# Waiting for the landing of each short run of indirect DMAs on GpSimd

## What is computed

```python
# layer 0: a gated message of each edge, summed by src
z = concat([x[src], x[dst], edge_attr], 1) @ W.T + b          # 106250 x 256
z = (z - mean(z, 0)) * rsqrt(var(z, 0) + eps) * gamma + beta   # over all edges
agg = zeros.at[src].add(sigmoid(z[:, :128]) * softplus(z[:, 128:]))
x1 = layernorm(x + (x + agg))
# layer 1: mean over the neighbours, by dst
local_mean = segment_sum(x1[src], dst) / max(count, 1)
fd = tanh(norm(x1 - local_mean))
h  = x1 + 0.2 * (relu(x1 @ W1 + b1) @ W2 + b2) * fd
out = layernorm(x1 + layernorm(h) * gamma1 + beta1)
```

## Time and profile before

| | |
|---|---|
| median of three runs | 3949.55 us (3946.03 to 3959.84) |
| span of the profiled execution | 5481.6 us, mean granted TensorE clock 0.784 |
| the profiled execution's time outside the span | not shown by the profile |
| busy | TensorE 3436.3 us, VectorE 2979.6, GpSimd 2626.3, ScalarE 2242.8 |
| scatters, line 367 | 830, at 66 to 1711 us |
| first gather, line 1245 | 272, at 3567 to 3951 us |
| second gather, line 1255 | 608, at 4249 to 5388 us |

### The profile page before, as it was taken

How to read it: one execution, slowest core, us unless ns; L and a number is a source line. 1 busy time by engine, 2 the same in 40 slices (tenths; PEclk the granted TensorE clock), 3 DMA queues, 4 the chain that set the end, 5 groups by cost and what they waited for, 6 DMA issues and landing times. The chain is left out here.

```text
span 5481.6 us, 84513 instructions
## 1 busy us (share of the span) xinstructions
PE 3436.3 (63%) x18854; PEld 2395.6 (44%) x18855; DVE 2979.6 (54%) x7781; ACT 2242.8 (41%) x6113; POOL 2626.3 (48%) x2634
## 2 busy tenths in 40 slices
PE   6745666666656888888888885661175555455542
PEld 2312222222223666666666664551165445445542
DVE  7975555555655333333333337971198555455547
ACT  1405555555654444444444448971197000000002
POOL 3775444444553555555555550077600544545542
PEclk8957777778877888888888887885587777777766
DMA  5322222122221666656666575463443221222213
GB/s 166 110 88 67 60 65 63 59 61 65 61 68 56 191 190 186 195 186 188 188 191 188 184 173 222 169 241 114 130 194 87 58 49 47 53 53 53 56 41 39
DMA packets 314711, 638.06 MB, mean 116 GB/s; under 512 B 54382, under 2 KB 188567, under 8 KB 306551
## 3 DMA queue, kind: packets, MB, share of 16 engines
q0 software_dynamic: 99440, 246.85, 16.9%
q1 hardware_dynamic: 172984, 266.76, 15.7%
q10 hardware_dynamic: 42192, 123.38, 6.1%
HBM read 424.53 MB, written 212.24 MB: 116 GB/s over the span
## 5 line engine op out<-in xcount | busy, mean ns | idle before, releaser
L367 POOL DMA_INDIRECT rec_d<-arena x830 | 887.8, 1070 | 815.8 <-issue 520.7
L853 POOL DMA_INDIRECT arena<-b_tab,arena x880 | 839.2, 954 | 730.4 <-DVE arena L874 405.8
L767 PE MATMUL psum<-arena 128*128 128x440 f16 x3360 | 776.5, 390 | 369.5 <-DVE arena L626 140.8
L626 DVE TENSOR_SCALAR arena<-iota_t,arena 128x880 f16<-128x880 f16 x840 | 516.1, 664 | 545.9 <-remote 320.5
L461 ACT ACTIVATE arena<-arena 128x128 f16<-128x128 f16 x1680 | 568.5, 388 | 469.9 <-remote 333.1
L767 PEld LDWEIGHTS psum<-arena 128*128 128x128 f16 x3360 | 344.2, 106 | 803.5 <-DVE arena L626 322.1
L1569 PE MATMUL psum<-arena,x_sb 128*128 128x129 f32 x2304 | 398.3, 347 | 454.2 <-DVE x_sb L1456 320.9
L964 PE MATMUL psum<-weT,arena 128*128 128x256 f32 x1760 | 627.6, 443 | 31.9 <-DVE arena L874 21.9
L1448 DVE TENSOR_TENSOR arena<-psum,arena 128x258 f32 x880 | 375.3, 426 | 476.9 <-remote 282.2
L1569 PEld LDWEIGHTS psum<-arena,x_sb 128*128 128x128 f32 x2304 | 375.7, 257 | 480.4 <-issue 192.3
L1255 POOL DMA_INDIRECT arena<-x_tab,arena x304 | 299.9, 987 | 556.1 <-DMA x_tab<-arena 295.9
(11 more groups left out here) (251 smaller groups left out, 5920.5 us busy)
## 6 DMA issues: line engine op xcount, KB each, us to landing
z_d<-arena ACTq DMA_DIRECT2D x220, 512.0 KB
arena<-z_d SPq DMA_DIRECT2D x44, 2560.0 KB
arena<-rec_d SPq DMA_DIRECT2D x220, 260.0 KB
arena<-in_edge_attr SPq DMA_DIRECT2D x83, 640.0 KB
arena<-early_d SPq DMA_DIRECT2D x34, 516.0 KB
arena<-b_tab,arena POOLq DMA_INDIRECT x880
rec_d<-arena POOLq DMA_INDIRECT x831
early_d<-arena POOLq DMA_DIRECT2D x9, 1032.0 KB
```

Of the source, the lines that this page charges most:

```text
L367: nc.gpsimd.indirect_dma_start(rec_rows, bass.IndirectOffsetOnAxis(e_idx[:, s, k:k + 1], 0), e_buf[:, s, k, :], None).then_inc(s_es[s], 16)
L626: nc.vector.tensor_scalar(hot_tile[:, s, :].rearrange("p (a b) -> p a b", b=TILE_RUN), iota_t[:, :, 0:TILE_RUN], tile_f[:, bass.ds(t, 1)], ...
L767: last = nc.tensor.matmul(bank(4 + 2 * k + h)[:, 0:HALF], hot_lane[:, s, k, :], hot_tile[:, s, h * HALF:(h + 1) * HALF], start=start, stop ...
L853: nc.gpsimd.indirect_dma_start(bg[:, s, k, :], None, b_tab, bass.IndirectOffsetOnAxis(rec[:, s, k, H:H + 1].bitcast(I32), 0)).then_inc(s_b ...
```

## The change

GpSimd gets waits on its own transfers. In part 1 it waits, before the first of a group's ten scatters, until the group before has landed entirely, and before the sixth until the first five have landed. In the first and the second gather it waits in the same way before the first and the fifth of a group's eight rows. Each wait asks for the full count of all DMAs of that semaphore so far, so nothing of GpSimd's is in the air when the next run of five, or of four, begins. The first three groups of scatters are taken out of the loop. Nothing else is changed, and the gather of the z stage isn't.

```diff
--- before.py
+++ after.py
@@ -359,18 +359,27 @@
                 nc.gpsimd.tensor_copy(identb[:], ident[:]).then_inc(s_const, 1)
                 pool.wait_ge(s_const, N_CONST + 2)
 
-                def scatter(it1, s):
+                RUN_IN = 5
+
+                def scatter(it1, s, first=False):
                     pool.wait_ge(s_el[s], it1 * 16)
                     pool.wait_ge(s_er[s], it1 * 3)
+                    if not first:
+                        pool.wait_ge(s_es[(s - 1) % IN_SLOTS], (it1 if s > 0 else it1 - 1) * (16 * G_IN))
                     settle(pool, s_turn)
                     for k in range(G_IN):
+                        if k == RUN_IN:
+                            pool.wait_ge(s_es[s], it1 * (16 * G_IN) - 16 * (G_IN - RUN_IN))
+                            settle(pool, s_turn)
                         nc.gpsimd.indirect_dma_start(rec_rows, bass.IndirectOffsetOnAxis(e_idx[:, s, k:k + 1], 0),
                                                      e_buf[:, s, k, :], None).then_inc(s_es[s], 16)
 
                 pool.wait_ge(s_tail0, 16)
                 pool.wait_ge(s_lz, 16 * len(LAST_BY_SP))
                 pool.wait_ge(s_lza, 16 * len(LAST_BY_ACT))
-                with pool.Fori(0, N_GROUPS_IN // IN_SLOTS) as it:
+                for s in range(IN_SLOTS):
+                    scatter(1, s, first=(s == 0))
+                with pool.Fori(1, N_GROUPS_IN // IN_SLOTS) as it:
                     for s in range(IN_SLOTS):
                         scatter(it + 1, s)
                 for g in range(N_GROUPS_IN // IN_SLOTS * IN_SLOTS, N_GROUPS_IN):
@@ -1131,6 +1140,7 @@
         x1e = flat[:, 0:EARLY_BLOCKS * (H + 1)].rearrange("p (b f) -> p b f", f=H + 1)
         x_ring2 = flat[:, 0:2 * G * (H + 1)].rearrange("p (s k f) -> p s k f", s=2, k=G)
         XS = 4
+        RUN = 4
 
         def ring_slot(s):
 
@@ -1242,6 +1252,9 @@
                     if g >= XS and g % 2 == 0:
                         pool.wait_ge(s_be[g // 2 % 2], g // XS * 16)
                     for k in range(G):
+                        if k % RUN == 0 and g + k > 0:
+                            before = g if k > 0 else g - 1
+                            pool.wait_ge(s_xe[before % XS], (before // XS + 1) * (16 * G) - (16 * (G - k) if k > 0 else 0))
                         nc.gpsimd.indirect_dma_start(ring_slot(g % XS)[:, k, :], None, x1_tab,
                                                      bass.IndirectOffsetOnAxis(l1_idx[:, g * G + k:g * G + k + 1], 0)).then_inc(s_xe[g % XS], 16)
                     if g >= 2 and g % 2 == 0:
@@ -1250,8 +1263,11 @@
                 for i in range(2):
                     pool.wait_ge(s_be[i], len(range(i, EARLY // 2, 2)) * 16)
 
-                def rows(s):
+                def rows(s, use):
                     for k in range(G):
+                        if k == RUN:
+                            pool.wait_ge(s_xe[s], use * (16 * G) + (EARLY_IN[s] - 16 * (G - RUN)))
+                            settle(pool, s_turn)
                         nc.gpsimd.indirect_dma_start(ring_slot(s)[:, k, :], None, x1_tab, bass.IndirectOffsetOnAxis(gi[:, s, k:k + 1], 0)).then_inc(s_xe[s], 16)
 
                 pool.wait_ge(s_xs, 48)
@@ -1263,15 +1279,19 @@
                         wait(pool, s_sg, 24 * (2 * use) + (8 * s - 80))
                     else:
                         wait(pool, s_sg, 24 * (2 * use) + (8 * s - 72))
+                    last = (s - 1) % XS
+                    pool.wait_ge(s_xe[last], (use if s > 0 else use - 1) * (16 * G) + EARLY_IN[last])
                     settle(pool, s_turn)
-                    rows(s)
+                    rows(s, use)
 
                 groups(pool, gather, None, 4 * ROUNDS, XS, head=XS)
                 for n in range(4 * ROUNDS, DIRECT):
                     pool.wait_ge(s_gi, n + 1)
                     before = n - XS
                     pool.wait_ge(s_sg, 8 * (3 * (before // 2) + 2 + before % 2 if before < 4 * ROUNDS else 2 * ROUNDS + before + 1))
-                    rows(n % XS)
+                    last = (n - 1) % XS
+                    pool.wait_ge(s_xe[last], ((n - 1) // XS + 1) * (16 * G) + EARLY_IN[last])
+                    rows(n % XS, n // XS + 1)
 
             @block.scalar
             def _(act):
```

## The result

The changed kernel takes 4752.12 us (median of four runs, 4747.16 to 4757.37) against 3947.79 for the kernel before: ratio 1.2051, 95% interval 1.2028 to 1.2073, slower by 804 us. The forecast was 4380, with a range to 4560; the sign was right and the size was not.

A forecast was written before the change was run, and what follows sets the result against it. The prediction took GpSimd as close to the bound, and as the bound in the average stage. Terms of 35 + 163 + 39 + 275 = 512 us gave 4461; between that and 4260 it forecast 4380 us, range 3850 to 4560.

The forecast's parts named there:

- sum of stages at the undisturbed pace: Whole kernel: busiest engine's time per stage, 3622 us, or 3966 with 10% idle added, 0.4% above the median.
- stalls without the profiler: Sign of a wrong prediction: VectorE's 10.5 us standstills in placement also without profiling; time then falls with the span.
- span between 5100 and 5500: Changed kernel's profiled execution: expected no longer than the 5481.6 us before, while a plain run gets longer.
- price of a wait: Every added wait: 2.09 us idle less the usual 0.30 gap, 1.79 us, from one gather row.
- cover of the scatters: Ranks and placement: ScalarE's 41 us a round and the ranks' pace hide part; 35 + 163 us come out.
- cover of the first gather: First gather: 435 us of messages and normalisation hide most of 474 us; 39 come out, bounds 0 and 72.
- term of + 275: Second gather, average stage: GpSimd is the bound, 76 groups take 1041 us against 766.
- Halving: Whole forecast: 4380 us, between 4461 at the profile's GpSimd pace and 4260 at a pitch nearer 1.10 us.
- All waits bare and dear: Rival, all 384 waits: 1.79 + 0.46 us at each, 864 us, 4810 in all; chance 0.03.
- The waits are covered: Rival, no change: pitch below 1.0 us and cheap landings hide the second gather's waits, 3950 us; chance 0.07.
- Cured stalls: Rival, faster: waits break GpSimd's long rows and cure stalls in the changed stages, 3825 to 3698 us; chance 0.20.

The follow-up runs named there:

- e0_before: The kernel before, unchanged, profiled once more: 3953.54 us, with a profiled span of 3946.0 us.
- e3: The kernel before with only the 152 waits in the second gather, two a group: 4296.97 us against 3956.49.
- e13: The kernel before with only one wait a group (76) in the second gather: 4121.45 us against 3955.73.
- e14: The kernel before with one wait a group in all three places, for the group before the last: 3953.31 us against 3955.73.
- e4: The kernel before with only one wait a group in the second gather, in a batch with stalls: 5253 us against 5471.58.
- e8: One wait a group in the second gather only, run in the other batch with stalls: 5301 us against 5296.41 for the kernel before.
- e9: The kernel before with one wait a group in all three places, for the group before the last, among stalls: 5502 us against 5296.41.
- e2_only_first: The kernel before with only the 67 waits in the first gather: 4120.87 us against 3956.49.

## Why the prediction came out as it did

**What a plain run is: half right.** The sum of stages at the undisturbed pace (3966) matched the median, and e0_before has no stalls anywhere, so the step from 5481.6 to 3950 was sound. That it matched to 0.4% was luck: I had the z stage at 1224 us (1102 over 0.9) where it takes 1121, and the average stage at 687 where it takes 771, and the two nearly cancel. The reading was wrong too: I called the difference the profiler's, and it is the execution's. The forecast named stalls without the profiler as a sign that it is wrong; some executions have them, those of the median don't. With that falls the expectation of a span between 5100 and 5500: it is 4755.6.

**The price of a wait: right for the scatters, too low for the gathers.** 1.79 us came from one row. Measured: 1.85 for the scatters (305 / 165), 2.24 in the second gather (340 / 152). There the landing row gives 2.06 to 2.08 of it and the rest, some 27 us in all, are idle times that I didn't trace one by one.

**The first step that failed: the cover of the scatters.** I gave a round of placement 41 us of ScalarE, against 38.2 of GpSimd, and took 163 + 35 us. In e0_before no scatter but one waits for ScalarE (0.3 us in all), and ScalarE waits for them instead. GpSimd's busy time in the two halves, ranks and placement (length, busy us, clock):

```profile
66.00:367.00 301.00, 243.25 (x186) 0.78 0.36 109
367.00:1210.00 843.00, 646.75 (x644) 0.97 0.35 99
```

With the gap of 0.30 behind each, 186 scatters of 1.31 us fill the first and 644 of 1.00 us the second. Three groups of placement take 39.3 us, and the 41 of ScalarE were 37 of work over an assumed 0.9. There was nothing to hide a wait under, not in the ranks either, where I had charged 35 us of 53. Each wait is bare: 305 us, 107 more than forecast.

**The second: the cover of the first gather.** I let 34 groups at 10.1 us run under 435 us of messages, so that 39 us came out. But beside working engines a gather is not 1.26 us: in e0_before 272 of them take 448 us. They end at 3074 us, while the stores of the last x1 were issued by 3030, and the second gather begins 7 us after their end. In e0_before's view of the line (duration ns min/median/max) the median is that of a quiet stage, and the longest ten times as much:

```profile
L1245 POOL DMA_INDIRECT arena<-x_tab,l_idx x144: 947/954/9813, 2626.4 to 3072.7; - x144
```

What the long ones have in common stands in the trace. When the longest starts, VectorE works on two operands in the chip's memory (line 1484):

```profile
3056.25 6.68 DVE L1484 TENSOR_TENSOR arena<-arena 128x6272 f32<-128x6272 f32 x1
3056.31 9.81 POOL L1245 DMA_INDIRECT arena<-x_tab,l_idx  x1 [0.31 <-issue]
```

All 24 others over 2.5 us lie beside an instruction of line 1380, which has two such operands too, and end 0.81 to 0.84 us after it. There was no cover at all, and beside the loads of z a landing took longer: 164 us, 125 more. The stalled profile hid both, as it had slowed just the engines that disturb a gather (VectorE 129 us busy in 385, against 396 in 448).

**The second gather: right in its mechanism.** GpSimd was the bound, at 771 us against my 766 and then 1120 against 1041; the term of + 275 was 340, by the price.

**Halving: wrong.** I averaged 4461 with a sum for a GpSimd pitch of 1.10 us, to mend 2.4% in my sum of stages. These 2.4% are 95 us, and they were the z stage's, which I had 103 us too long. GpSimd's usual pitch is 1.27 and 1.26 in e0_before as in the profile before, and with the long descriptors its mean is higher, 1.38 for the scatters and 1.65 in the first gather (its 17 stores included). So "0.95 + 0.30 at every one of some 2500 DMAs", with which I argued against the rival of covered waits, was not what the trace had. The halving took off 81 us. With 107, 125 and 65 the four make 378 of the 372 us by which I was low.

**The rivals.** "All waits bare and dear" (4810, to which I gave 0.03) is the one that came about, at 2.09 us a wait instead of 2.25. "The waits are covered" fell: e3 and e13. "Cured stalls" fell for executions without stalls, e14 above all; for those with stalls its mechanism was seen in one stage (e4 and e8), and whether the changed kernel gains there stays open, as it never ran in such a batch. What makes an execution stall stays open too. The runs show only that it lasted for a whole batch, and each batch has one chip.

**The Trainium skill's rule held.** The Trainium skill ("DMA: Bandwidth & Descriptors", "Rules for kernel authors") advises to wait late on a DMA's semaphore. The fixed cost of about 2.0 us that the same page gives for a GpSimd DMA ("Anatomy of one DMA — SWDGE (gpsimd) path") made 768 us for 384 waits, an estimate; 804 were measured. Another page of the Trainium skill, "SBUF — State Buffer" (section "SBUF: two separate sides"), says that a VectorE instruction with two inputs in SBUF, the chip's memory, holds a pair of ports for its whole length against a GpSimd instruction that reads SBUF. The long descriptors beside line 1380 agree with it, 24 of the 25 over 2.5 us in e0_before. The timeline of the changed kernel has them as well; no run here takes VectorE's work away to show it.

```profile
3021.97 2.82 DVE L1400 SCALAR_TENSOR_TENSOR arena<-arena 128x2560 f32<-128x2560 f32 x1 [1.04 <-ACT arena L1323]
...
3022.06 3.56 POOL L1258 DMA_INDIRECT arena<-x_tab,l_idx  x1 [0.30 <-issue]
```

## What to carry to other kernels

When a profile's span is far from the time, profile again before pricing anything: a second profile of the same kernel would have put right three of the four terms. An engine with no idle time but its fixed gaps is the bound. Here every wait on its own transfer then cost the full landing, in proportion to the count, and a wait for the group before the last was free. Whether there are only fixed gaps is read from the mean over a stage, not from a few regular rows: the earlier trace rows had 229 us for 177 descriptors where a row has 0.97 each. Cover is to be read from a trace in which the covering work runs at its real pace, since that work also slows what it covers.

## What the runs showed of the hardware

- A landing waited out by the issuer adds 1.85 us to a scatter into DRAM, 2.2 to a gather into the chip's memory, and up to 6.4 us of idleness was seen beside loads of 2.5 MB; the scatters' writes into DRAM were not the dearer ones.
- A gather's descriptors, 0.95 us else, took 2.5 to 3.8 us beside a VectorE instruction of 2.8 us with two operands in the chip's memory, and ended 0.82 us after it (24 in e0_before, 20 in e2_only_first).
- Some executions have stalls of up to 10.5 us on VectorE and ScalarE in placement while GpSimd issues indirect DMAs without a break (and again in e9's profile): 5208 to 5490 us for a kernel that takes 3950. Such times were there in two batches, each on a chip of its own, from the first run to the last. The gaps between GpSimd's scatters stay at 0.30 us meanwhile.
